# Graph attention kernel: each gather issued on GpSimd waits for the landing of the gather two before it

## The reference

```python
for l in range(L):                                   # L = 2
    xn = _layernorm(x, ln1_g[l], ln1_b[l])
    xp = xn + xn @ Wpos[l] + bpos[l] + deg[:, None] * Wdeg[l][0] + bdeg[l]
    q, k, v = (xp @ W[l] + b[l]).reshape(n, H, HD)    # for Wq, Wk, Wv
    att = einsum('ehd,ehd->eh', q[dst], k[src]) / scale      # clipped to +-50, nan to 0
    ex = exp(att - segment_max(att, dst)[dst])
    alpha = ex / (segment_sum(ex, dst)[dst] + 1e-16)
    aggr = segment_sum(v[src] * alpha, dst)
    x = x + (aggr @ Wo[l] + bo[l])
    x = x + gelu(_layernorm(x, ln2_g[l], ln2_b[l]) @ W1[l] + b1[l]) @ W2[l] + b2[l]
out = _layernorm(x_in + x)
```

## Time and profile before

| | |
|---|---|
| median of 3 runs | 2100.44 us (2098.3 to 2102.22) |
| span of the profiled execution | 3221.0 us |
| time of the profiled execution itself | none is given beside its span |
| granted TensorE clock, mean over the span | 0.694 |
| POOL busy | 1486.6 us, 46% |
| PE busy | 1677.5 us, 52% |
| DVE busy | 1445.7 us, 45% |
| DMA | 322.97 MB, 100 GB/s over the span |

### The profile page before, as it was taken

One profiled execution on the slowest core, in us unless ns is written; L12 is line 12 of the kernel. 1 busy time (PEld: TensorE's weight loads), 2 busy tenths in 40 slices (PEclk: granted clock), 3 DMA queues, 4 the chain that ended last, 5 costly groups with the idle time before them and its releaser, 6 DMA issues.

```text
span 3221.0 us, 44116 instructions
## 1 busy us (share of the span) xinstructions
PE 1677.5 (52%) x11693; PEld 1432.5 (44%) x11694; DVE 1445.7 (45%) x2484; ACT 910.1 (28%) x1616; POOL 1486.6 (46%) x1584
## 2 busy tenths in 40 slices
PE   7444444355566556555343534444456565556545
PEld 5344334345455445444333433343445454545444
DVE  8634434344444535454363434343444444434435
ACT  3212212123333323332131212122233233323322
POOL 0545444545444444544534445444544444444452
PEclk9667676767666777775666767676677667666667
DMA  2423333323323333333323333233333333333332
GB/s 74 136 85 109 95 99 97 105 93 113 97 95 105 108 99 96 114 105 97 116 72 101 102 95 107 90 102 98 102 103 104 103 93 98 110 98 99 101 119 75
DMA packets 120301, 322.97 MB, mean 100 GB/s; under 512 B 31459, under 2 KB 43684, under 8 KB 120170
## 3 DMA queue, kind: packets, MB, share of 16 engines
q0 software_dynamic: 75072, 205.10, 21.5%
q1 hardware_dynamic: 44292, 115.07, 10.7%
q10 hardware_dynamic: 838, 1.60, 0.2%
HBM read 313.45 MB, written 9.73 MB: 100 GB/s over the span
## 4 chain that ended last, share of the span: by engine, by line
another core or an unknown queue 29%; DVE 21%; issue 20%; PE 15%; DVEq 11%; ACT 2%; ACTq 0%; DMA 0%; POOL 0%; POOLq 0%
PE ps L1352 8%; DVE dots L1082 5%; DVEq L359 4%; PE ps L1337 4%; DVE msg L1106 4%; DVE prod L1072 3%; DVEq L393 2%; DVE hot L992 1%; DVEq L992 1%; DVE acc L987 1%; PE ps L1314 1%; DVEq L987 1%; DVE not_nan L1084 1%; DVE q_parts L839 1%
## 5 line engine op out<-in xcount | busy, mean ns | idle before, releaser
L566 POOL DMA_INDIRECT kv<-kv_tab,src_idx x1564 | 1482.8, 948 | 1697.8 <-DVE msg L1106 1131.3
L1352 PE MATMUL ps<-msg,hot 128*128 128x136 f32 x3896 | 783.3, 366 | 766.4 <-DVE acc L987 459.0
L1352 PEld LDWEIGHTS ps<-msg,hot 128*128 128x128 f32 x3896 | 705.0, 264 | 827.5 <-issue 531.8
L1337 PE MATMUL ps<-q_parts,hotT 128*128 x5844 | 545.4, 251 | 608.3 <-issue 436.6
L1337 PEld LDWEIGHTS ps<-q_parts,hotT 128*128 x5844 | 449.5, 113 | 717.5 <-issue 700.3
L1072 DVE TENSOR_TENSOR prod<-kv,ps 128x1024 f32<-128x1024 f32 (+1 forms) x198 | 238.1, 1202 | 608.3 <-remote 431.3
L705 ACT ACTIVATE hotT<-dist 128x1024 bf16 x246 | 259.9, 1057 | 535.0 <-remote 388.1
L992 DVE SCALAR_TENSOR_TENSOR hot<-dst_col,neg_base,ps 128x1024 f32<-128x1024 f32 (+1 forms) x246 | 311.8, 1267 | 144.4 <-issue 141.0
L702 ACT ACTIVATE dist<-dst_rows,neg_node 128x1024 bf16<-128x1024 int32 x246 | 282.4, 1148 | 146.1 <-issue 135.5
L987 DVE TENSOR_TENSOR acc<-acc,ps 128x136 f32 x246 | 71.3, 290 | 553.7 <-remote 316.1
L1082 DVE TENSOR_REDUCE dots<-prod 128x64 f32<-128x1024 f32 (+1 forms) x198 | 238.8, 1206 | 33.3 <-DVE prod L1072 24.2
(11 more groups left out here) (215 smaller groups left out, 995.4 us busy)
## 6 DMA issues: line engine op xcount, KB each, us to landing
dst_rows<-in_dst SPq DMA_DIRECT2D x194, 512.0 KB
kv<-kv_tab,src_idx POOLq DMA_INDIRECT x1564
kv_tab<-qkv SPq DMA_DIRECT2D x25, 128.0 KB
kv_tab<-qkv SPq DMA_DIRECT2D x3, 768.0 KB, 3.8
out_tab<-z SPq DMA_DIRECT2D x24, 64.0 KB
out<-out_tab SPq DMA_DIRECT2D x1, 1498.5 KB, 7.2
hot<-in_L_gnn_W SPq DMA_DIRECT2D x2, 256.0 KB
w<-in_L_gnn_W SPq DMA_DIRECT2D x2, 256.0 KB
```

Source lines behind the costliest of these rows:

```text
L566: pool.indirect_dma_start(kv[:, u, c, :], None, kv_tab[l][:, :], bass.IndirectOffsetOnAxis(ap=src_idx[:, c, at(g)], axis=0)).then_inc(kv_i ...
L1337: last = MM(qd[:, c * P:(c + 1) * P], hotT[:, bass.ds(pr % 2, 1), c * P:(c + 1) * P], q_parts[:, at(t), k * D:(k + 1) * D], start=first an ...
L1352: last = MM(agg, hot[:, u % 2, c, :], msg[:, u % 2, c, :], start=(c == 0), stop=(c == nch - 1))
```

## The change

```diff
+LANES = 2
...
-        kv_in = [sems(f"kv_in{l}_", SLOTS) for l in range(L)]
+        kv_in = [sems(f"kv_in{u}_", LANES) for u in range(SLOTS)]
...
+        def landed(l, u, turn, n):
+
+            before = l * sum(chunks_of(g) for g in range(u, NG, SLOTS)) // LANES
+            return before + GC // LANES * turn + n
+
...
+            def await_landing(l, g, c):
+
+                pool.wait_ge(kv_in[g % SLOTS][c % LANES], 16 * landed(l, g % SLOTS, g // SLOTS, c // LANES + 1))
+
...
                     for c in range(chunks_of(g)):
+                        if c >= LANES:
+                            await_landing(l, g, c - LANES)
+                        elif g:
+                            await_landing(l, g - 1, chunks_of(g - 1) - LANES + c)
                         pool.indirect_dma_start(kv[:, u, c, :], None, kv_tab[l][:, :],
-                                                bass.IndirectOffsetOnAxis(ap=src_idx[:, c, at(g)], axis=0)).then_inc(kv_in[l][u], 16)
+                                                bass.IndirectOffsetOnAxis(ap=src_idx[:, c, at(g)], axis=0)).then_inc(kv_in[u][c % LANES], 16)
...
-                    dve.wait_ge(kv_in[l][u], 16 * (GC * i + nch))
+                    for lane in range(LANES):
+                        dve.wait_ge(kv_in[u][lane], 16 * landed(l, u, i, nch // LANES))
```

## The result

| | before | after |
|---|---|---|
| median | 2099.48 us (4 runs) | 2867.84 us (4 runs, 2862.76 to 2871.92) |
| ratio, with its 95% interval | | 1.3659, 1.3639 to 1.368 |
| span of the profiled execution | 3221.0 us | 2867.7 us |

The change makes the kernel slower by 768 us. The direction was forecast, by the mechanism that the experiments bear out, but 469 us were forecast: the time lies above the range.

What follows compares the result with a forecast made beforehand. The prediction took POOL's rate of issuing gathers, 1.25 us each, as the bound. From 2100 us, + 484 us for the waits (cadence 1.56) and - 15 us given back made 2569 us, range 2310 to 2690.

Steps and rivals of the forecast that it cites:

- bound by POOL's issue rate: Kernel before: gathers start 1.25 us apart, 10.0 us per group, above what VectorE and TensorE need.
- "remote" stretches: VectorE's 931.6 us in 84 unnamed waits of the first profile, taken as a recording cost absent from timed runs.
- VectorE's double wait: VectorE's single waiting instruction names two semaphores instead of one: claimed to cost 0.
- The sum's loop: Gather start to landing 2.59 us plus landing to next start 0.53: 3.12 us for two gathers, cadence 1.56, + 484 us.
- The loop without a load: Lone gather of 128 KB: 2.40 us from start to landing, then 0.53 us from landing to next start.
- The loads: 512 KB loads beside gathers: about 2 of 8 gathers land 0.75 us later, 0.19 us in the mean.
- Wait counts on POOL: A group's first gather has two kinds of wait, one behind the other; the earlier landing is the later event: 0.
- The 15 us given back: POOL's wait when the four slots are first full, shortened by 7.5 us in each layer: - 15 us.
- sum of 2112: Kernel before, paced by POOL: 87.0 us to first gather, 1955 us of gathers, 35 between layers, 35 behind the last.
- short loop: Rival: recorder's cost per packet missing in timed runs, loop at the lower bound or less; 2150 to 2300 us; chance 0.13.
- Hidden: Rival: slack covers the waits, needing a loop of 2.5 us or less; no change, 2100 us; chance 0.05.
- faster: Rival: two gathers under way disturb loads and engines less, from the second group on; at most 2088 us; chance 0.03.

Runs made afterwards that it cites:

- second profile: The kernel before, unchanged, captured again: measured 2096.46 us, with POOL waiting 2.1 us for VectorE and no "remote" waits.
- swapped order: The changed kernel with the two waits of a group's first gather in the other order, landing first in the code, slot second: 2836.16 us.
- one under way: The changed kernel with gather n waiting for gather n-1, so that no gathers overlap: 5203.63 us, ratio to before 2.4821.

## Why the prediction was wrong in size

- **That the timed kernel is bound by POOL's issue rate although the profile says the opposite: right.** The second profile has 1555 gathers with the bare gap, and leaving out gathers speeds the kernel up. That the "remote" stretches cost timed runs nothing was right as well; that they come with profiling was not: the second capture has none.
- **VectorE's double wait, 0: right** (2097.43 us).
- **The sum's loop, 3.12 us, is the term that was too small: it measured 3.50.** In the changed kernel a gather reached its semaphore after 3.07 us in the mean (groups 6 to 95), and 0.43 us later the gather that waited for it started; half of the sum is the cadence of 1.75. Of the 0.38 us that were missing, three parts:
  - *The loop without a load*, 2.40 + 0.53 = 2.93 us. Measured 3.00: the last packet at 2.40 as read from rows 6 and 7, 0.34 to the semaphore, 0.26 to the next start. Low by 0.07, about 55 us. This part was nearly right.
  - *The loads, 0.19 us of mean landing, 148 us.* The landings were longer by 3.07 - 2.74 = 0.33 us, that is 0.14 more than forecast, about 110 us. The gather beside the load took 4.23 us and the next one 3.47, 1.5 and 0.7 more than alone, where the prediction had 0.75 for each of the two. Cutting the loads gave back 207 us, and the cut loads were not gone.
  - *Nothing between a landing and the next start but the release.* "Wait counts on POOL ... 0" failed, and so did taking the lanes for always ready to take turns: 0.43 - 0.26 = 0.17 us, about 130 us. I took the later event to hide the other wait at a group's border. What it costs is not an event but the form, the landing's wait standing alone ahead of the gather: 32 us by the swapped order. The rest is a landed gather that has to wait for POOL to get past the other lane (the even or the odd gathers); it is read from the traces, no run takes it away by itself.
- Together 55 + 110 + 130 = 295 us of the 299 missed. The 15 us given back for the filling of the slots do not exist: in the second profile POOL waits for VectorE 2.1 us in all, so the 15.1 us of the earlier trace rows belonged to the stretched capture. What the change did give back is some 7 us outside of the gathers, 23.2 us instead of 26.7 between the layers and 21.2 instead of 23.4 behind the last one's start. The ends of 35 us in the sum of 2112 came from that capture as well.
- **The rivals.** The short loop was wrong in sign: the loop is longer than recorded packets say. Hidden and faster are out. The Trainium skill's rule (DMA: Bandwidth & Descriptors, Anatomy of one DMA — SWDGE (gpsimd) path: a fixed 2.0 us plus bytes, by estimate 2.3 us here) is below the 2.74 us that the gather took to its semaphore with one under way; the measurement decides. That the fixed part does not shrink with the transfer no run here shows, since all gathers have one size; that an added wait lays the whole way to the semaphore bare is shown, 2.7 of 3.0 us with one under way.
- **The signs that I named:** starts at 1.45 to 1.65 us in the mean were short of 1.75; the idle time is put down to a DMA, as named; POOL's busy time is the same to 0.1 us. That the profiled span would grow by under 100 us was wrong, it fell by 353 us: I took the stretched capture for a property of profiling.

## To carry to other kernels

A wait for a landing before each DMA turns a latency that nobody sees into a rate: with D under way, cadence is at least loop / D, and to be hidden it needs room for the longest landings beside other traffic, not for the mean; here 3.0 / 2 against 1.25 was hopeless, and even 3.0 / 4 lost 2.4%, half of it by the order of two waits. Where pacing is wanted, give each transfer under way its own semaphore, and let the transfer carry the wait that comes last. In these programs it carried the one that the code has first; the other stood alone ahead of it. And when a profile's span is far above the timed runs, trust the durations of short instructions, rebuild the bound from them, and take a second capture before believing its waits or its longer stretches.

## What was not expected of the hardware

- Two captures of one program: 3221.0 and 2094.3 us, with runs at 2096 to 2100 us. In the long one VectorE stood 931.6 us in unnamed waits; the gather's 0.95 us and its gap of 0.30 were right, and so was VectorE's `prod` (1202 against 1206 ns); TensorE's matmul of L1352 (366 against 336 ns) and the stretch between the layers (36.0 against 26.7 us) were not.
- An always met second wait on a gather costs 270 us over 1310 gathers.
- One 512 KB load per group costs at least 207 us or nothing, depending on whether the gathers' landings are waited for.
